# Gathered rows multiplied four at a time on VectorE and summed by ScalarE's accumulator

## What is computed

```python
q = norm(x) @ w_q                  # batch-normalised, 8 heads, two halves of 128
sim = q . keys                     # 128 scores a half; top 8 of each half
all_scores = sx[:, None] + sy[None, :]           # 64 sums a head, top 8 of them: 64 picks a token
wd, wu = down_embed[indices], up_embed[indices]  # 512 numbers each
h = gelu(sum_d(x * wd)) * softmax(scores)
out = sum_k(h * wu)
```

## Time and profile before

| | us |
|---|---|
| median of 3 runs | 3695.06 |
| the profiled execution | 3666.36 |
| its span, first to last instruction | 3664.6 |
| TensorE matmul, busy | 3022.0 (82%) |
| VectorE, busy | 2333.9 (64%) |
| GpSimd, busy | 2059.6 (56%) |
| ScalarE, busy | 990.9 (27%) |

### The profile page before, as it was taken

One profiled execution on the slowest core, in us unless ns is written; L12 is line 12 of the kernel. 1 busy time (PEld: TensorE's weight loads), 2 busy tenths in 40 slices (PEclk: granted clock), 3 DMA queues, 4 the chain that ended last, 5 costly groups with the idle time before them and its releaser, 6 DMA issues.

```text
span 3664.6 us, 36576 instructions
## 1 busy us (share of the span) xinstructions
PE 3022.0 (82%) x8870; PEld 1516.7 (41%) x8870; DVE 2333.9 (64%) x8191; ACT 990.9 (27%) x2805; POOL 2059.6 (56%) x2193
## 2 busy tenths in 40 slices
PE   8999999688787787878788878788888787888867
PEld 6787756333333333333333333333333333333323
DVE  5777735466666676666666656666666665666664
ACT  1222201222222232322223222232232222322322
POOL 1111131466666666666666666666666666666665
PEclk9999999898898998989998989888899898999988
DMA  5111100699999999999999999999999999999998
GB/s 189 55 57 60 49 17 24 260 365 360 367 367 361 377 349 370 363 368 366 364 374 358 366 367 368 363 364 371 366 358 368 365 364 366 359 365 364 364 374 318
DMA packets 324648, 1132.02 MB, mean 309 GB/s; under 512 B 36187, under 2 KB 36827, under 8 KB 323880
## 3 DMA queue, kind: packets, MB, share of 16 engines
q0 software_dynamic: 294912, 1073.87, 77.3%
q1 hardware_dynamic: 28800, 55.92, 4.4%
q10 hardware_dynamic: 808, 0.99, 0.1%
HBM read 1113.87 MB, written 16.78 MB: 309 GB/s over the span
## 4 chain that ended last, share of the span: by engine, by line
DVE 37%; issue 25%; another core or an unknown queue 12%; PE 5%; ACT 3%; POOL 2%; DVEq 0%; DMA 0%; POOLq 0%; ACTq 0%
DVE rows L1123 23%; DVE expert_top_i L966 3%; PE expert_out_ps L1366 2%; DVE expert_top_s L959 2%; POOL rows L872 2%; DVE expert_hid L1123 1%; DVE expert_best_i L991 1%; PE expert_out_ps L1286 1%; ACT expert_diag L1214 1%; ACT expert_keys_sb L1214 1%; DVE expert_onehot L1027 1%; DVE expert_best L985 1%; DVE expert_picked L1037 1%; DVE expert_onehot L1033 1%
## 5 line engine op out<-in xcount | busy, mean ns | idle before, releaser
L872 POOL DMA_INDIRECT rows<-in_table,expert_idx x2048 | 1934.1, 944 | 1098.7 <-issue 605.9
L1123 DVE CUSTOM_DVE_ANT_0 rows<-rows,expert_xn_ps 128x512 f32<-128x512 f32 x2048 | 1329.2, 679 | 450.2 <-issue 290.6
L1366 PE MATMUL expert_out_ps<-rows,expert_diag 128*128 128x512 f32 x2048 | 1017.7, 655 | 362.2 <-ACT expert_diag L1214 273.8
L1366 PE MATMUL expert_out_ps<-rows,expert_keys_sb 128*128 128x512 f32 x2048 | 963.0, 626 | 218.8 <-ACT expert_keys_sb L1214 183.7
L1366 PEld LDWEIGHTS expert_out_ps<-rows,expert_diag 128*128 128x128 f32 x2048 | 426.0, 211 | 942.9 <-issue 710.1
L1366 PEld LDWEIGHTS expert_out_ps<-rows,expert_keys_sb 128*128 128x128 f32 x2048 | 405.3, 201 | 747.3 <-issue 532.9
L1222 ACT ACTIVATE expert_act_h<-expert_hid 128x8 f32<-128x8 f32 x256 | 53.4, 209 | 1639.5 <-DVE expert_hid L1123 762.5
L1351 PE MATMUL expert_score_ps<-amat,expert_xnT 128*128 128x512 f32 x992 | 465.1, 592 | 1.3 <-ACT expert_score_ps L1204 1.3
L1214 ACT ACTIVATE expert_keys_sb<-ident,expert_coef 128x128 f32<-128x128 f32 x1024 | 313.1, 388 | 255.5 <-remote 106.2
L1214 ACT ACTIVATE expert_diag<-ident,expert_coef 128x128 f32<-128x128 f32 x1024 | 313.0, 388 | 219.4 <-remote 102.0
L1351 PEld LDWEIGHTS expert_score_ps<-amat,expert_xnT 128*128 128x128 f32 x992 | 188.4, 190 | 238.4 <-issue 236.7
(11 more groups left out here) (132 smaller groups left out, 1979.1 us busy)
## 6 DMA issues: line engine op xcount, KB each, us to landing
rows<-in_table,expert_idx POOLq DMA_INDIRECT x2048
x_t<-in_x SPq DMA_DIRECT2D x32, 256.0 KB, 2.9
attention_xr_t<-in_x SPq DMA_DIRECT2D x32, 256.0 KB, 2.7
x_dram<-rows SPq DMA_DIRECT2D x32, 256.0 KB, 2.0
expert_x_t<-x_dram SPq DMA_DIRECT2D x32, 256.0 KB
out_y<-expert_x_t SPq DMA_DIRECT2D x32, 256.0 KB
rows<-in_w_q SPq DMA_DIRECT2D x4, 1024.0 KB, 7.1
rows<-in_w_qT SPq DMA_DIRECT2D x4, 1024.0 KB, 9.3
```

The lines of the kernel that those rows point to most:

```text
L872: pool.indirect_dma_start(rows[:, slot, :], None, table[:, :], bass.IndirectOffsetOnAxis(ap=idx[:, par, h * TOP + k:h * TOP + k + 1], axis ...
L1123: dot = dve.tensor_tensor_reduce(down, down, xn_ps[:, par, :], 1.0, 0.0, ALU.mult, ALU.add, hid[:, h % 4, k:k + 1])
L1366: mm = pe.matmul(out_ps[:, par, :], diag(h)[:, k, :], rows[:, (h % 4) * TOP + k, D:2 * D], start=(h == 0 and k == 0), stop=(h == PH - 1 an ...
```

## The change

The unit of the chain becomes a half head, 4 rows, 16 a tile, with one semaphore a group of 4 slots. VectorE multiplies the four down halves of a group by the tokens in one instruction, back into `rows`. ScalarE sums each product with a copy in place and the accumulator (`sums_of_products`), then takes gelu of the four sums. VectorE makes the coefficients of half head j-1 behind the products of j, and ScalarE the diagonals of j-1 ahead of the sums of j. The diagonals, sums, gelus and coefficients lie in rings of four half heads. The places are used as integers, without the two casts of `float_places`; the self-waits on `early_done` in the tile go, and the pieces of the choice get new places, one or two behind each product. The second half's indices of a tile move into the tile itself. Seeds, turned rows and score matmuls move with them. Context lines and renamed views that say nothing more are left out.

```diff
@@ -56,6 +56,9 @@
 NG = len(CHUNK_GROUPS)
 SLOTS = 32
 HALF = TOP // 2
+HALVES = NPICK // HALF
+GROUPS = SLOTS // HALF
+RING = 4
...
-    diag_own = sb("diag", [P, 2, TOP, P])
...
+    diag = sb("diag", [P, RING, HALF, P])
...
                     .then_inc(ev["rs_done"], 1)
             def step(t, par, half):
-                for h in range(PH):
-                    if h % 4 == 0:
-                        wait(pool, "idx_done", t * 2 + h // 4 + 1)
-                    for k0 in range(0, TOP, HALF):
-                        free = t * 16 + (2 * h + k0 // HALF) + 1 - 8
-                        if not isinstance(free, int) or free > 0:
-                            pool.wait_ge(ev["up_done"], free)
-                        if isinstance(t, int) and t == 0 and h == 3:
-                            wait(pool, "amat_done", NM)
-                        pool.sem_inc(issued, 1)
-                        for k in range(k0, k0 + HALF):
-                            slot = (h % 4) * TOP + k
-                            pool.indirect_dma_start(
-                                rows[:, slot, :], None, table[:, :],
-                                bass.IndirectOffsetOnAxis(
-                                    ap=idx[:, par, h * TOP + k:h * TOP + k + 1], axis=0))\
-                                .then_inc(row_in[slot], 16)
+                for j in range(HALVES):
+                    if j % GROUPS == 0:
+                        wait(pool, "idx_done", t * 2 + j // GROUPS + 1)
+                    free = t * HALVES + j + 1 - GROUPS
+                    if not isinstance(free, int) or free > 0:
+                        pool.wait_ge(ev["up_done"], free)
+                    if isinstance(t, int) and t == 0 and j == 6:
+                        wait(pool, "amat_done", NM)
+                    pool.sem_inc(issued, 1)
+                    for k in range(j * HALF, (j + 1) * HALF):
+                        pool.indirect_dma_start(
+                            rows[:, k % SLOTS, :], None, table[:, :],
+                            bass.IndirectOffsetOnAxis(ap=idx[:, par, k:k + 1], axis=0))\
+                            .then_inc(row_in[j % GROUPS], 16)
...
-                    ins = dve.max_index(top_i[:, m * TOP:(m + 1) * TOP],
+                    h = m // 2
+                    ins = dve.max_index(top_i[:, h // HH, m % 2, h % HH, :],
...
-            flat_places = where_f[:, :, :].rearrange("p a n -> p (a n)")
+            flat_places = where_i[:, :, :].rearrange("p a n -> p (a n)")
...
-            def float_places(d):
-                dve.tensor_copy(where_f[:, :, :], where_i[:, :, :])
-                return dve.tensor_copy(top_if[:, :, :, :], i4[:, :, d * HH:(d + 1) * HH])
...
-            def keep_marked():
+            def keep_marked(d):
+                places = top_i[:, d].rearrange("p a h j -> p (a h) j")
                 return dve.tensor_tensor(onehot4, onehot4,
-                                         places4.unsqueeze(2).to_broadcast([P, PH, TOP, TOP]), ALU.mult)
+                                         places.unsqueeze(2).to_broadcast([P, PH, TOP, TOP]), ALU.mult)
...
-            def coefficients(t, par, h):
-                wait(dve, "gelu_done", t * PH + h + 1)
-                dve.tensor_tensor(coef[:, h % 4, :], act_h[:, h % 4, :],
-                                  prob[:, par, h * TOP:(h + 1) * TOP], ALU.mult)\
+            def products(par, j):
+                slot = j % GROUPS * HALF
+                down = rows[:, slot:slot + HALF, 0:D]
+                return dve.tensor_tensor(
+                    down, down, xn_ps[:, par, :].unsqueeze(1).to_broadcast([P, HALF, D]), ALU.mult)
+            def coefficients(t, par, j):
+                wait(dve, "gelu_done", t * HALVES + j + 1)
+                dve.tensor_tensor(coef[:, j % RING, :], act_h[:, j % RING, :],
+                                  prob[:, par, j * HALF:(j + 1) * HALF], ALU.mult)\
                    .then_inc(ev["coef_done"], 1)
...
+            def step(t, par, half, more, first):
+                for j in range(HALVES):
+                    dve.wait_ge(row_in[j % GROUPS], half * 256 + (par * 2 + j // GROUPS + 1) * 64)
+                    made_products = products(par, j)
+                    if first and j == 0:
+                        made_products.then_inc(ev["multiplied"], 1)
+                    if j in (4, 6, 11, 14) and more >= 2:
+                        wait(dve, "scored", (t + 2) * NQ + (4, 6, 11, 14).index(j) + 1)
+                    if j > 0:
+                        coefficients(t, par, j - 1)
+                    elif not first:
+                        coefficients(t - 1, 1 - par, HALVES - 1)
+                    if j == 0:
+                        if more >= 1:
+                            top_places(3)
+                    if j == 1:
+                        if more >= 1:
+                            split_places(0)
+                        if not first:
+                            indices(par, 1)
+                    if j == 2 and more >= 1:
+                        pair_sums(1)
+                    if j == 3 and more >= 1:
+                        mark_places()
+                    if j == 4:
+                        if more >= 2:
+                            top_values(0)
+                        if more >= 1:
+                            pair_best(1)
+                    if j == 5:
+                        if more >= 1:
+                            keep_marked(0)
+                        if not first:
+                            finish(t - 1, 1 - par, half + par - 1)
+                    if j == 6:
+                        if more >= 2:
+                            top_values(1)
+                        if more >= 1:
+                            pair_places(1)
+                            shift_best()
+                    if j == 7:
+                        if more >= 2:
+                            top_places(0)
+                        if more >= 1:
+                            pick_marked()
+                    if j == 8 and more >= 1:
+                        split_places(1)
+                        norm_again(t + 1, 1 - par, half + par)
+                    if j == 9:
+                        if more >= 2:
+                            top_places(1)
+                        if more >= 1:
+                            indices(1 - par, 0)
+                    if j == 10 and more >= 1:
+                        mark_places()
+                        exp_sum()
+                    if j == 11 and more >= 2:
+                        top_values(2)
                         pair_sums(0)
+                    if j == 12:
+                        if more >= 1:
+                            keep_marked(1)
+                            exp_inverse()
+                        if more >= 3:
+                            norm(t + 3, 1 - par, half + par + 1)
+                    if j == 13 and more >= 2:
                         pair_best(0)
+                    if j == 14 and more >= 2:
+                        top_values(3)
+                        top_places(2)
+                    if j == 15:
+                        if more >= 1:
+                            pick_marked()
+                            weights(1 - par)
+                        if more >= 2:
+                            pair_places(0)
...
             wait(dve, "topped", NQ + 2)
             now(pair_sums(0))
             now(pair_best(0))
+            now(pair_places(0))
+            top(1, 2)
+            wait(dve, "scored", 2 * NQ)
+            now(top_values(3))
             norm(2, 0, 1)
             run(dve, step)
-            coefficients(NT - 1, 1, PH - 1)
+            coefficients(NT - 1, 1, HALVES - 1)
...
-            def diagonals(t, par, h):
-                wait(act, "coef_done", t * PH + h + 1)
-                wait(act, "up_done", t * 16 + 2 * (h - 3))
-                for k in range(TOP):
-                    ins = act.activation(diag(h)[:, k, :], ident[:, :], ACT.Copy,
-                                         scale=coef[:, h % 4, k:k + 1])
-                    if k % HALF == HALF - 1:
-                        ins.then_inc(ev["diag_done"], 1)
+            def sums_of_products(j):
+                for k in range(HALF):
+                    down = rows[:, j % GROUPS * HALF + k, 0:D]
+                    ins = act.activation(down, down, ACT.Copy, accum_out=hid[:, j % RING, k:k + 1])
+                ins.then_inc(ev["summed"], 1)
+            def diagonals(t, j):
+                wait(act, "coef_done", t * HALVES + j + 1)
+                wait(act, "up_done", t * HALVES + j + 1 - RING)
+                for k in range(HALF):
+                    ins = act.activation(diag[:, j % RING, k, :], ident[:, :], ACT.Copy,
+                                         scale=coef[:, j % RING, k:k + 1])
+                ins.then_inc(ev["diag_done"], 1)
             def step(t, par, half, more, first):
-                for h in range(PH):
```

(56 more changed lines are left out.)

102 lines of the change are left out of this document (9 added, 93 removed).

## The result

The changed kernel takes 3739.43 us (median of 4 runs, 3733.93 to 3746.62) where the kernel before takes 3693.7: 1.0129 of before, 95% interval 1.0101 to 1.0158. Slower, where 3577 was forecast. Later runs gave 1.0116 (1.0081 to 1.015) on one chip and 0.9965 (0.9951 to 0.9979) on another, where the kernel before takes 3397 us. Why both are true is what the experiments are about.

What follows compares the result with a forecast made beforehand. VectorE's crawl by instruction count under a full DMA was taken to delay slots and stall GpSimd. From 93.3 to 89.5 us a tile, 3.8 less on 31 tiles, -118 us: 3695 - 118 = 3577 us, range 3380 to 3820.

Steps and rivals of the forecast that it cites:

- The bound: Steady tiles, 93.3 us each: VectorE crawls while the DMA is full, slots come late, GpSimd stalls 13.5 us a tile.
- Dots: VectorE's 16 long products a tile replace 64 multiplies and 64 accumulator reads: 2.23 us each, 3.4 us a tile saved.
- Sums: ScalarE's 64 new accumulating copies a tile: 0.65 us each (0.51 to 0.81), ScalarE 75.5 us a tile, hidden by GpSimd's 79.5.
- Rival B: ScalarE's price: at 0.81 us a sum it needs 85.7 us a tile, 95.7 in all; 3770 us, chance 0.16.
- Waits: VectorE's wait for four landed rows costs 0; GpSimd's wait for the next tile's first indices 0 to 1.7 us a tile.
- The sum: Per tile: the 13.8 us lost scaled by 0.315/0.54 to 8.0, then 2.0 given back: 89.5 us, -118 us in all.
- C: The crawl moves to ScalarE with 216 instructions a tile, perhaps by instruction fetch: 96.5 us a tile, 3794 us, chance 0.15.
- D: Nothing net: stalls belong to the full DMA, however few VectorE's instructions; 93 us a tile, 3695 +-15, chance 0.14.
- Ends: Start and end of the kernel: +6 us before the first product, -7 us from the shorter half-head chain; put at 0.

Runs made afterwards that it cites:

- half_bytes: Changed kernel with gathers of 2 KB a row instead of 4 KB, the up half of the rows not fetched, on chip 6: 3260.22 us.
- after_3: Changed kernel, unchanged, run again on chip 12, which has no late steps: 3386.02 us, 0.9965 of the kernel before.
- tiny_act_before_3: Kernel before with 16 one-element copies added on ScalarE ahead of each head's gelu, on chip 10, with late steps: 3717.1 us, 1.0076.
- tiny_act: Changed kernel with six one-element copies added on ScalarE ahead of each half head's sums, on chip 7: 4034.54 us, 1.0917 of the kernel before.
- tiny_act_before_2: Kernel before with 16 one-element copies added on ScalarE ahead of each head's gelu, on chip 12, without late steps: 3396.07 us.
- diag_dve: Changed kernel with a half head's four diagonals made by VectorE in one instruction, none on ScalarE, on chip 7: 3699.37 us, 1.0005 of the kernel before.
- half_matmuls_3: Changed kernel without the matmuls of rows 1 and 3 of each half head, on chip 10, with late steps: 3859.64 us, 1.046 of the kernel before.

## Why the prediction was wrong, step by step

**The bound.** Here the prediction failed first. It read the pace rightly (93.3 us a tile, stalls for slots, VectorE at one instruction in 0.7 us while the DMA is full), and then put the two together: VectorE crawls, rows are not used up, GpSimd stalls. The rows did not show this link. In the kernel before the rows of a stalled slot had mostly been used up: 400 of the 433 us of stalls come after the matmuls waited for, when TensorE's `up_done` is late, by up to 18.1 us. Matmuls that ended late, for which VectorE can be the reason, end the other 33 us, 1 us a tile of the 13.8 that were to be scaled. Nor was it seen that all this belongs to some chips: on the others the gathers alone set 85 us a tile.

**Dots.** The product was put at 2.23 us from start to start; it takes 2.28, busy. VectorE's instructions were to be 124 a tile; 657 in 500 us at 95.4 us are 125, so the casts and coefficients were counted right too. GpSimd's 79.5 us a tile came out at 81.0 in half_bytes, where nothing else holds it.

**Sums.** Taken at 0.65 us (0.51 to 0.81); they start 0.61 us apart (2078.99, 2079.60, 2080.21). The accumulator's read of 187 ns ends under the next sum and adds 0.10 us to a plain copy's 0.51. Undisturbed, ScalarE has 399.77 us in 500 to do, at 84.6 us a tile (2047 gathers from 640.00 to 3347.01 in after_3) 67.6 us, where 75.5 was the sum with waits. Rival B falls with it: ScalarE's busy share is 0.72 and not above 0.9. Its other sign, VectorE waiting for act_h, is there all the same, the largest wait of VectorE's: a sign that two causes share.

**Waits.** Put at 0 to 1.7 us, from full-speed durations. The way of `up_done` from TensorE to GpSimd has no term at all; it is where the 400 us lie. The wait for its own sums was put at 0.12 us; undisturbed the gap is 0.03, but in the changed kernel it averages 276.3/335 = 0.82, and single ones last 8 to 9 us. This term was too small too: 16 x 0.8 = 13 us a tile on ScalarE, which had 79.5 - 75.5 = 4 us of room by the sum. Most of it lies in time in which the gathers run or wait for TensorE's step anyway; the rest of the stalls grew by 53 us, 1.7 us a tile.

**The sum.** Here the wrong link became a number. The sum scaled all 13.8 us of a tile by VectorE's instructions, 0.54 to 0.315, and got 5.8 us back. The part that doesn't hang on VectorE stayed, 400 us before and 399 after, so nothing came back. The sum also took ScalarE as running at full speed in a full DMA, since its eight diagonals at 2022.85 did. They did at 0.85 instructions a us; at 2.2, in tiny_act_before_3, 35 of 224 diagonals were late. With ScalarE at 2.26 in the changed kernel its sums are late, and that is how the rest came from 33 to 86 us. So the forecast missed the gain by the first error and the loss by the second.

**Rivals.** C's number is the nearest, 96.5 us a tile and 3794 us against 95.4 and 3739, and in part by luck: it scales the same 13.8 us, most of which isn't ScalarE's or VectorE's. It had the engine and the count of what the change added, and the wrong cause, which the version without a loop took away. It was given 0.15 for want of a row that shows an engine with fewer than 1.4 instructions a us as untouched because of that; both engines' counts stood in the earlier trace rows. The sign named for C, instructions 0.7 us apart, is rare in the changed kernel (tiny_act shows it); the late step before gelu is how it looks with fewer instructions.

D said that the stalls belong to the full DMA, however few instructions VectorE has. Of VectorE this is right: 400 us stayed. It was 44 us low, for what ScalarE added. Of instructions in general it isn't: TensorE's part is 85 us with half of its matmuls, and the copies of one element raise the rest. On chips 6 and 12 the full DMA does set the time, with no late step.

**Ends.** Put at 0. The first gather and the last lie 2707.0 us apart in after_3 and 2720.7 in tiny_act_before_2 (638.55 to 3359.26), so its gain of 11 us lies in the steady part, at 400 GB/s for 398. In the first pair the stretch behind the last gather grew from 19.9 to 32.7 us, on chip 0 from 25.9 to 26.9.

No version that computes the same is faster than both kernels on both kinds of chip. Nearest is the one with VectorE's diagonals: level with before where steps are late (1.0005), 0.3% faster where they aren't, as is the changed kernel there.

## What to carry to other kernels

A slow stretch of one engine beside a stall of another isn't yet its cause. Take the stall, find the instruction whose step it waits for, and look when that instruction ended: if long before, the step is late, and relieving the engines ahead of it may give nothing back, as here. Where a DMA queue is kept full, count each engine's instructions per microsecond, as well as its busy time, before work is moved to it; six short instructions cost four times as much as a long one of the same time here. And before a trace's stalls are priced, look whether they are the kernel's or the chip's: here the same kernel took 3397 us on two chips and 3667 to 3698 on three.

## What the runs showed of the hardware

- On three chips of five, with the DMA at 411 to 412 GB/s (mean of the full windows), instructions of ScalarE and VectorE often start 0.70 us apart, or a multiple of it (2031.14 to 2033.24; tiny_act), and their semaphore steps arrive up to 9.7 us after the instruction's end. ScalarE and VectorE had no late step at 0.85 to 1.32 instructions a us, and had some in every kernel with 1.49 (diag_dve's VectorE) or more, up to 3.0. No kernel lies between; 1/0.70 = 1.43 does. The longest lateness of a sum in the changed kernel, 8.9 us, would be 13 instructions of 0.70: an estimate of what can queue.
- On these three chips TensorE did as many matmuls in full windows as in the others (9.9 and 9.9 in 5 us, kernel before, 3.5 instructions a us), but its steps came up to 18.1 us late: 400 of the 433 us of GpSimd's stalls. At 2.0 instructions a us it is 85 us (half_matmuls_3).
- On the other two chips, with full windows at 410 GB/s, nothing of this. What tells the chips apart isn't known. Their traces have every semaphore step's record; those of the three lack mostly 20 to 50% of them. All times here are of executions that left a trace. The Trainium skill says of the unit that writes such records ("NOTIFIC — the notification-queue block", section "7.1 Overflow: three behaviours, one of which stalls the engine") that its internal pipeline always holds its producers back rather than lose a record, which could stall an engine. No run here shows that it is this unit or whether its records are why steps are late, and whether a run without a trace has late steps stays open.
- With VectorE's diagonals, 128x512 from SBUF to SBUF, a gather's instruction on GpSimd took 990 ns instead of 944 (diag_dve), and 981 instead of 951 on chip 12.
